# A decoder layer on one core: masked maximum on VectorE instead of a mask matmul, and a new order of VectorE's, ScalarE's and GpSimd's turn

## The chip, the core and the metric

The program runs on one core of one Trainium2 chip. A core has a matrix engine (TensorE, "PE" in the rows, with its weight loads as "PEld"), a vector engine (VectorE, DVE), a scalar engine (ScalarE, ACT), GpSimd (POOL) and a sync engine (SP) that only issues transfers here. The engines run side by side, each works through its own instructions in order, and they wait for one another by semaphores. The metric is the device time of one execution in microseconds.

## The reference

The input is `x` of 2 x 1024 x 512. The layer is an attention block and a gated feed-forward block, each between two layer norms and a residual:

```
xn = layernorm(x)                       # 2048 rows of 512
q = xn @ Wq (32 heads x 128); k, v = xn @ Wk, xn @ Wv (8 heads x 128, each shared by 4 q heads)
o_lin = gla_scan(softmax(q), softmax(k), v, logsigmoid(k)/16)    # linear attention with decay
y = sliding window attention (64 back, in blocks of 64, positions rotated), masked softmax
o = bf16(0.5*y + 0.5*o_lin) @ Wo;  x = x + layernorm(o)
w1, w2, w3 -> NF4 quantised and dequantised, in blocks of 64 with their absolute maximum
h = silu(xn @ w1') * (xn @ w2');  x = x + layernorm(h @ w3')
```

The masked softmax sets scores outside the window to minus infinity, takes each row's maximum, subtracts it, and normalises the exponentials by their sum.

## The kernel before

The 2048 rows are 16 tiles of 128. One **turn** handles one tile and one k/v head with its 4 q heads, so there are 128 turns, in 32 groups of four; `p` = 0, 1, 2, 3 is the turn's place in its group. Groups 0 to 3 and 28 to 31 are written out, groups 4 to 27 are the body of a loop. After the turns comes the feed-forward block, which the change leaves alone.

Each engine has a function `turn(t)` that writes its instructions in a fixed order; it works on turn t and also on pieces of the turns before (`l1` = t-1, `l2` = t-2, `l3` = t-3). `wait_tile(engine, semaphore, turn, back)` is the wait for a turn's step.

TensorE's order in a turn: `project_kv(t)`, `decays_and_krT(l1)`, `project_out(l3)`, `gla_scores(l2)`, `turn_q(l1)`, `inter_and_update(l2)`, `probabilities(l2)`, `scores(l1)`, `project_q(t)`, `qsT_and_ktT(l1)`, `output(l2)`. `scores` first writes the window's mask (0 or -1e30) into the bank SC by a matmul of `win` with an identity, and adds the four score products to it. `project_kv(t)` overwrites the bank PKV, and waits for `kabs_ev` and `gl_d` of turn t-1, the last reads of that bank.

VectorE's order in a turn: `use_k(t)` (maximum, minimum with zero and rotation of k), `q_sums(l1)`, `gla_k(l1)`, `merge(l2)`, `add_out(l3)`, `state(l2)`, `p_max(l1)` (the maximum of the scores, once `scores` is done), `log_decay(t)` (writes `gh` and PKV), `low_decay(t)` (writes `gl`, signals `gl_d`), the NF4 work, `p_sums(l1)`, `use_q(t)`, `gla_q(l1)`.

The NF4 work turns the feed-forward weights into quantised ones, one piece of 128 x 512 per group. `nf4_blocks` finds the maximum of each block of 64 and its reciprocal; `nf4` divides (`f_nrm`) and then writes 15 steps `f_s[k % 8]` = (f_nrm > bound_k) * delta_k; GpSimd adds the 15 steps up in `f_acc` (`nf4_add`, one turn later); `nf4_end` scales the sum. `NF4_STEPS` says which k come in which turn of a group.

GpSimd's order in a turn: `rotate_q(l1)`, `rotate_k(t)`, `softmax_q(l1)`, `nf4_add(l1)`, `softmax_p(l1)`, `split_low` (the low halves of the next weights; the 512-wide one where p = 3).

ScalarE copies banks out and takes exponentials; of its order the change touches `q_exps(l1)` (exponentials of q, needed by `project_q(t)`) and `decays(l1)` (needed by `gla_k`, signals `dec_ev`).

Of the kernel before, what the change touches and what calls it, by code (L numbers as in the profile page):

```python
# [45 lines left out]
NF4_STEPS = (range(0, 2), range(2, 6), range(6, 11), range(11, 15))  # L46
# [63 lines left out]
def layer(nc, x, wq, wk, wv, wo, wf, cosc, sinc, winmask, causal, cumsum, identc, keepc, dq, out):  # L110
# [15 lines left out]
    with ExitStack() as whole:  # L126
# [10 lines left out]
        def sb(name, shape, dt=F32):  # L137
# [76 lines left out]
        rp = sb("rp", [P, 2, GRP])  # L214
        f_max = sb("f_max", [P, 2, NF4_MAX // BLK])
# [30 lines left out]
            rp_d pm_d pa_ev su_d em_d sr_d acc_d qrope_p krope_p qn_p pn_p  # L246
# [198 lines left out]
        def _(pool):  # L445
# [31 lines left out]
            def nf4_add(t):  # L477
                w = width_of(t.i)
                for k in NF4_STEPS[t.p]:
# [16 lines left out]
            def turn(t):  # L496
# [24 lines left out]
            nf4_add(last_turn)  # L521
# [23 lines left out]
        def _(act):  # L545
# [20 lines left out]

            def q_exps(t):
# [12 lines left out]
            def decays(t):  # L580
# [7 lines left out]
                nc.scalar.activation(edT[:, r, :], SM[:, P:P + 130], ACT.Exp)  # L588
                nc.scalar.activation(ked, ked, ACT.Exp, scale=-1.0).then_inc(s["dec_ev"], 1)
# [101 lines left out]
            def turn(t):  # L691
# [13 lines left out]
                k_exps(t)  # L705
                if n == 0:
# [103 lines left out]
        def _(dve):  # L810
# [30 lines left out]

            def low_decay(t):
# [188 lines left out]
            def turn(t):  # L1031
                l1, l2, l3, n = t.back(1), t.back(2), t.back(3), number(t)
                use_k(t)
                if l1.real():
                    q_sums(l1)
# [35 lines left out]
                if t.p == 0:  # L1071
                    nf4(t)
# [76 lines left out]
            state(l2)  # L1149
# [30 lines left out]
        def _(pe):  # L1180
# [84 lines left out]
            def scores(t):  # L1265
# [4 lines left out]
                nc.tensor.matmul(SC[:], identb[:], win[:, 1, :] if t.p else win[:, t.i % 2, :], start=True, stop=False)  # L1270
                low = 1 - r
                for b in range(2):
# [3 lines left out]
                    for hp in range(2):  # L1276
# [3 lines left out]
                                                start=False, stop=(j == 3))  # L1280
# [167 lines left out]
def constants():  # L1448
# [37 lines left out]
    keep = np.ones((P, 2), np.float32)  # L1486
    keep[:, 0] = 0.0
# [21 lines left out]
```

## Time and profile before

| | |
|---|---|
| time, median of 3 runs | 1959.39 us (1958.69 to 1960.08) |
| the profiled execution, its own time | 1959.31 us |
| its span from the first to the last instruction | 1957.5 us |
| busy in the span: PE, DVE, ACT, POOL | 1876.3, 1433.4, 1229.4, 1235.9 us |
| granted TensorE clock, mean | 0.99 |

The whole execution is 1.8 us longer than its span. A busy figure is the time in which at least one instruction of an engine was under way. A timeline row gives the start, how long the instruction (or a merged run of "xN" of them) was under way, the engine, the line of the kernel, the operation, what it writes and reads, and in brackets an idle time ahead of it with what ended that. Successive instructions of an engine overlap: what one costs its engine is the distance to the next start, not its own length. A TensorE product of two fp32 operands shows as two matmul records.

### The profile page before, as it was taken

The page shows a single profiled execution, that of the slowest core. Times are in us where ns is not written, and L with a number is a line of the kernel's source. Part 1 is how long each engine was busy: PE and PEld are TensorE (multiplying, and loading weights), DVE is VectorE, ACT ScalarE, POOL GpSimd, SP SyncE. Part 2 cuts the span into 40 slices and gives each one's busy share as a digit, 9 for nine tenths or more (in the row PEclk, how much of TensorE's full clock was granted, in tenths as well). Part 3 has the DMA queues.
Part 4 walks back from the last instruction along what each step waited for, and adds up shares of the span by engine and source line. Part 5 has one row for each costly group of instructions (what it writes and reads, how often), then busy time and mean ns, then how long its engine had stood idle before and what let it go on. Part 6 is the DMA issues. An engine that isn't in the chain of part 4 may idle for free.

```text
span 1957.5 us, 42161 instructions
## 1 busy us (share of the span) xinstructions
PE 1876.3 (96%) x11698; PEld 1252.8 (64%) x11698; DVE 1433.4 (73%) x3926; ACT 1229.4 (63%) x4840; POOL 1235.9 (63%) x1150
## 2 busy tenths in 40 slices
PE   4999999999999999999999999999989979999997
PEld 3667677777777777776777676777666635444443
DVE  6998888888888888888888888888899644302022
ACT  5777777777777777777777777776666535312121
POOL 3777777777777777777777777777677521212121
PEclk8999999999999999999999999999999989999999
DMA  5000000000000000000000000000100042000000
GB/s 199 25 26 25 26 25 24 24 24 24 32 25 24 24 24 24 29 24 24 24 24 24 30 29 24 24 24 13 54 13 7 7 134 79 26 1 22 0 21 21
DMA packets 44353, 61.43 MB, mean 31 GB/s; under 512 B 4928, under 2 KB 18496, under 8 KB 44288
## 3 DMA queue, kind: packets, MB, share of 16 engines
q1 hardware_dynamic: 44288, 60.64, 9.6%
q8 instruction: 32, 0.52, 0.1%
q14 instruction: 33, 0.27, 0.0%
HBM read 47.97 MB, written 12.65 MB: 31 GB/s over the span
## 4 chain that ended last, share of the span: by engine, by line
PE 62%; DVE 16%; issue 14%; POOL 3%; ACT 2%; DVEq 1%; DMA 0%; SPq 0%; POOLq 0%; ACTq 0%
PE bank L1250 18%; PE bank L1239 8%; PE bank L1278 6%; PE bank L1221 4%; PE bank L1294 4%; PE bank L1315 4%; PE bank L1379 3%; PE bank L1287 3%; DVE f_s L963 2%; PE bank L1205 2%; PE bank L1304 2%; POOL hl L527 2%; DVE f_nrm L953 2%; PE bank L1270 1%; PE bank L1297 1%
## 5 line engine op out<-in xcount | busy, mean ns | idle before, releaser
L488 POOL TENSOR_TENSOR f_acc<-f_acc,f_s 128x512 f32<-128x512 f32 (+1 forms) x416 | 534.3, 1284 | 30.6 <-POOL f_acc L488 0.4
L1250 PE MATMUL bank<-wh,xh 128*128 (+2 forms) x1024 | 334.9, 327 | 7.3 <-DVE cumh L1099 6.2
L1250 PE MATMUL bank<-wl,xh 128*128 (+2 forms) x1024 | 335.0, 327 | 0.0
L1250 PE MATMUL bank<-wh,xl 128*128 (+2 forms) x1024 | 334.7, 327 | 0.0
L469 POOL TENSOR_TENSOR pr<-pr,rp 128x512 f32<-128x512 f32 x128 | 133.0, 1039 | 229.5 <-DVE rp L894 229.5
L963 DVE TENSOR_SCALAR f_s<-f_nrm 128x512 f32<-128x512 f32 (+1 forms) x480 | 240.9, 561 | 3.7
L575 ACT ACTIVATE qe<-bank,nqm 128x128 f32<-128x128 f32 x512 | 180.8, 365 | 80.3 <-DVE qs L823 57.2
L527 POOL TENSOR_TENSOR hl<-hf,hh 128x512 f16<-128x512 f32 (+1 forms) x44 | 50.8, 1155 | 283.7 <-ACT hh L754 283.7
L1379 PE MATMUL bank<-xh,w 128*128 (+3 forms) x704 | 224.8, 382 | 3.8 <-ACT sg L748 3.8
L603 ACT ACTIVATE pr<-bank,pmx 128x128 f32<-128x128 f32 x512 | 180.9, 367 | 37.5 <-DVE pmx L887 29.6
L1239 PE MATMUL bank<-wh,oT 128*128 (+1 forms) x512 | 194.0, 379 | 3.8 <-DVE xl L1019 1.4
L1239 PE MATMUL bank<-wl,oT 128*128 (+1 forms) x512 | 194.0, 379 | 0.0
L1109 DVE SCALAR_TENSOR_TENSOR hf<-bank,sg 128x512 f32<-128x512 f32 (+1 forms) x44 | 30.4, 690 | 215.8 <-PE bank L1379 203.3
L594 ACT ACTIVATE qrT<-bank 128x512 f32<-128x512 f32 x128 | 76.4, 597 | 170.1 <-PE bank L1205 170.1
L451 POOL TENSOR_TENSOR qc<-qc,qs 128x512 f32<-128x512 f32 x128 | 162.9, 1273 | 23.3 <-DVE qs L823 23.3
L456 POOL TENSOR_TENSOR kc<-kc,ks 128x128 f32<-128x128 f32 x128 | 72.2, 564 | 117.0 <-DVE ks L823 117.0
L1250 PEld LDWEIGHTS bank<-wh,xl 128*128 (+1 forms) x1024 | 100.5, 98 | 66.9 <-issue 0.8
L1250 PEld LDWEIGHTS bank<-wl,xh 128*128 (+1 forms) x1024 | 100.5, 98 | 66.5 <-issue 0.6
L887 DVE TENSOR_REDUCE pmx<-bank 128x4 f32<-128x512 f32 x128 | 88.2, 689 | 73.1 <-PE bank L1278 73.1
L1250 PEld LDWEIGHTS bank<-wh,xh 128*128 (+1 forms) x1024 | 100.8, 98 | 61.6 <-issue 8.9
L1278 PEld LDWEIGHTS bank<-krT,qrT 128*128 128x128 f32 x1024 | 135.3, 193 | 4.9
L1278 PE MATMUL bank<-krT,qrT 128*128 128x128 f32 x1024 | 135.8, 276 | 0.0
(177 smaller groups left out, 4973.7 us busy)
## 6 DMA issues: line engine op xcount, KB each, us to landing
f_raw<-wf SPq DMA_DIRECT2D x30, 256.0 KB, 2.6
dequantised<-f_dq SPq DMA_DIRECT2D x30, 256.0 KB, 2.0
wt<-dequantised SPq DMA_DIRECT2D x30, 256.0 KB, 3.0
raw_qkv<-wq SPq DMA_DIRECT2D x29, 256.0 KB, 2.5
raw_o<-wo SPq DMA_DIRECT2D x29, 256.0 KB, 2.6
rows<-x SPq DMA_DIRECT2D x4, 1024.0 KB, 9.3
xr<-x SPq DMA_DIRECT2D x16, 256.0 KB, 3.6
out<-yo SPq DMA_DIRECT2D x16, 256.0 KB, 2.1
```

Source lines behind the costliest of these rows:

```text
L451: nc.gpsimd.tensor_tensor(qc[:, r, :], qc[:, r, :], qs[:, r, :], ALU.add).then_inc(s["qrope_p"], 1)
L469: nc.gpsimd.tensor_tensor(v, v, rp[:, r, :].unsqueeze(2).to_broadcast([P, GRP, P]), ALU.mult).then_inc(s["pn_p"], 1)
L488: nc.gpsimd.tensor_tensor(f_acc[:, 0:w], f_acc[:, 0:w], f_s[:, k % 8, 0:w], ALU.add)\
L527: nc.gpsimd.tensor_tensor(hl[0:n, c % 2, :], hf[0:n, c % 2, :], hh[0:n, c % 2, :], ALU.subtract)\
L575: last = nc.scalar.activation(qe[:, r, h * P:(h + 1) * P], PQ[:, h * P:(h + 1) * P], ACT.Exp, bias=nqm[:, r, h:h + 1], scale=1.0 / WSCALE, ...
L603: last = nc.scalar.activation(pr[:, r, j * P:(j + 1) * P], SC[:, j * P:(j + 1) * P], ACT.Exp, bias=pmx[:, r, j:j + 1], accum_out=psm[:, r, ...
L887: nc.vector.tensor_reduce(pmx[:, r, :], SC[:].rearrange("p (h n) -> p h n", h=GRP), AX.X, ALU.max, negate=True).then_inc(s["pmx_d"], 1)
L963: nc.vector.tensor_scalar(f_s[:, k % 8, 0:w], f_nrm[:, 0:w], float(BOUND[k]), float(DELTA[k]), ALU.is_gt, ALU.mult).then_inc(s["f_sd"], 1)
L1239: last = nc.tensor.matmul(PW[:], oT[:, t.p % 2, h].rearrange("p b n -> p (b n)"), w[:, sl + h, QW + KVW:WW], start=(h == 0 and k == 0), st ...
L1250: last = nc.tensor.matmul(dst, av, w[:, sl + c, lo:hi], start=(n == 0), stop=(n == 3 * NC - 1))
L1278: last = nc.tensor.matmul(SC[:, j * P:(j + 1) * P], qrT[:, r, b, 2 * hp:2 * hp + 2, :].rearrange("p h n -> p (h n)"), keys, start=False, s ...
L1379: last = nc.tensor.matmul(dst[0:n, :], w12[c][:, ww, "gu".index(kind), d, 0:n], x4, start=(k == 0), stop=(k == 3 * NC - 1))
```

## The change

1. TensorE no longer multiplies the mask into SC. The first score product starts the bank. VectorE's `p_max` is no longer one reduction over 128 x 512 but, after a one-element memset, four instructions over 128 x 128 that each compute `-(scores + mask)`, write it back to SC and keep the smallest value as `pmx`; each comes with a read-out of that value. ScalarE's exponential then uses scale -1. In turns with p = 0 the mask of the first two heads is `win0`, a copy that ScalarE makes in the same turn (`head_mask`).
2. VectorE's turn: `q_sums(l1)` moves behind `add_out`; `state(l2)` is cut in two, and `state_scale` moves behind `p_max`; the reciprocal of k's sums (`k_sums`) moves from `gla_k(l1)` to the turn before; `low_decay(t)` moves behind `nf4(t)`; `nf4_blocks(i + 1)` comes in the turn with p = 1 of group i, and `nf4` of the turn with p = 0 takes the same place as in the others.
3. `em`, the factor that clears the state where a sequence starts, is made by ScalarE's exponential with a bias, not by a VectorE product.
4. ScalarE: `decays(l1)` ahead of `q_exps(l1)`.
5. GpSimd: the first two additions of `nf4_add(l1)` ahead of `softmax_q(l1)`.
6. `NF4_STEPS` becomes 2, 3, 5, 5 steps in place of 2, 4, 5, 4.

```diff
-NF4_STEPS = (range(0, 2), range(2, 6), range(6, 11), range(11, 15))
+NF4_STEPS = (range(0, 2), range(2, 5), range(5, 10), range(10, 15))
...
                 if l1.real():
+                    nf4_add(l1, NF4_STEPS[l1.p][:2])
                     softmax_q(l1)
-                    nf4_add(l1)
+                    nf4_add(l1, NF4_STEPS[l1.p][2:])
                     softmax_p(l1)
...
+            def head_mask(t):
+                if t.p == 0:
+                    nc.scalar.activation(win0[:], win[:, t.i % 2, 0:P], ACT.Copy).then_inc(s["head_mask"], 1)
...
                 nc.scalar.activation(edT[:, r, :], SM[:, P:P + 130], ACT.Exp)
+                if t.p == 0 and not (isinstance(t.i, int) and t.i == 0):
+                    nc.scalar.activation(em[:, 0, :], SM[:, 2 * P:2 * P + 1], ACT.Exp,
+                                         bias=keep[:].unsqueeze(2)[:, t.i % 2, :])
...
 -                                                bias=pmx[:, r, j:j + 1],
+                                                bias=pmx[:, r, j:j + 1], scale=-1.0,
...
                 if l1.real():
+                    decays(l1)
                     q_exps(l1)
-                    decays(l1)
...
+            def k_sums(t):
+                r = t.p % 2
+                wait_tile(dve, s["ke_ev"], t)
+                nc.vector.reciprocal(rks[:, r, :], ksum[:, r, :]).then_inc(s["rks_d"], 1)
...
-                nc.vector.tensor_reduce(pmx[:, r, :], SC[:].rearrange("p (h n) -> p h n", h=GRP), AX.X, ALU.max,
-                                        negate=True).then_inc(s["pmx_d"], 1)
+                nc.vector.memset(pause[:], 0.0)
+                for j in range(GRP):
+                    sl = slice(j * P, (j + 1) * P)
+                    mask = win[:, 1, sl] if t.p or j >= 2 else win0[:]
+                    last = nc.vector.tensor_tensor_reduce(SC[:, sl], SC[:, sl], mask, -1.0, -MASKED, ALU.add,
+                                                          ALU.min, pmx[:, r, j:j + 1])
+                last.then_inc(s["pmx_d"], 1)
...
                 use_k(t)
-                if l1.real():
-                    q_sums(l1)
...
+                if l1.real():
+                    q_sums(l1)
                 if l2.real():
-                    state(l2)
+                    state_sum(l2)
                 if l1.real():
                     p_max(l1)
+                if l2.real():
+                    state_scale(l2)
                 log_decay(t)
+                k_sums(t)
+                if t.p == 0 and isinstance(t.i, int) and t.i == 0:
+                    nf4_blocks(0)
+                nf4(t)
                 low_decay(t)
-                if t.p == 0:
-                    nf4_blocks(t.i)
-                else:
-                    nf4(t)
+                if t.p == 1 and not (isinstance(t.i, int) and t.i == STEPS - 1):
+                    nf4_blocks(t.i + 1)
...
-                nc.tensor.matmul(SC[:], identb[:], win[:, 1, :] if t.p else win[:, t.i % 2, :], start=True, stop=False)
+                if t.p == 0:
+                    pe.wait_ge(s["head_mask"], t.i + 1)
...
-                                                start=False, stop=(j == 3))
+                                                start=(j == 0), stop=(j == 3))
```

VectorE from `state` to `p_sums` in a turn that has five steps, before (`sr` is the scaled state, `pmx` the maximum, `gh` and `gl` the high and low half of the log decay, `f_s` the NF4 steps, `rp` the reciprocal of the probabilities' sums):

```order
L911 TENSOR_TENSOR bank<-bank,sr 128x128 [waits s_u_done]
L922 TENSOR_SCALAR sr<-bank,edT 128x128 [waits s_su_d,s_dec_ev]
L887 TENSOR_REDUCE pmx<-bank 128x4 [waits s_sc_done]
L839 TENSOR_TENSOR gh<-bank,kabs 128x128 [waits s_small_done,s_kneg_d,s_l1_ev]
L840 TENSOR_TENSOR bank<-bank,kabs 128x128
L845 TENSOR_TENSOR gl<-bank,gh 128x128 [waits s_g_d]
L963 TENSOR_SCALAR f_s<-f_nrm 128x512 [waits s_f_ad] x5
L894 RECIPROCAL rp<-psm 128x4 [waits s_pn_p,s_p_exp]
```

And in the changed kernel, in the same kind of turn, from the third of the four masked maxima on:

```order
L907 ISA pmx 128x1
L907 ISA bank,pmx<-bank,win 128x128
L907 ISA pmx 128x1
L944 TENSOR_SCALAR sr<-bank,edT 128x128 [waits s_su_d,s_dec_ev]
L851 TENSOR_TENSOR gh<-bank,kabs 128x128 [waits s_small_done,s_kneg_d,s_l1_ev]
L852 TENSOR_TENSOR bank<-bank,kabs 128x128
L857 RECIPROCAL rks<-ksum 128x1 [waits s_ke_ev]
L985 TENSOR_SCALAR f_s<-f_nrm 128x512 [waits s_f_ad] x5
L862 TENSOR_TENSOR gl<-bank,gh 128x128 [waits s_g_d]
L915 RECIPROCAL rp<-psm 128x4 [waits s_pn_p,s_p_exp]
```

`gl` stood three rows behind the maximum and ahead of the five steps. It now stands behind them, and `sr` and `rks` stand between the maximum and the steps.

GpSimd's turn with p = 0 before (`kc` and `qc` are rotations, `qe` is the normalised exponentials of q, `pr` those of the scores, `f_acc` the NF4 sum):

```order
L456 TENSOR_TENSOR kc<-kc,ks 128x128 [waits s_krope_d]
L462 TENSOR_TENSOR qe<-qe,rq 128x512 [waits s_rq_d]
L488 TENSOR_TENSOR f_acc<-f_acc,f_s 128x512 [waits s_f_ad,s_f_sd] x4
L469 TENSOR_TENSOR pr<-pr,rp 128x512 [waits s_rp_d]
L475 TENSOR_TENSOR wl<-raw_qkv,wh 128x256 [waits s_wqk_hi]
```

And after:

```order
L453 TENSOR_TENSOR qc<-qc,qs 128x512 [waits s_qrope_d]
L458 TENSOR_TENSOR kc<-kc,ks 128x128 [waits s_krope_d]
L490 TENSOR_TENSOR f_acc<-f_acc,f_s 128x512 [waits s_f_ad,s_f_sd] x2
L464 TENSOR_TENSOR qe<-qe,rq 128x512 [waits s_rq_d]
L490 TENSOR_TENSOR f_acc<-f_acc,f_s 128x512 [waits s_f_ad,s_f_sd] x3
L471 TENSOR_TENSOR pr<-pr,rp 128x512 [waits s_rp_d]
```

Two additions stand ahead of `qe`, three behind it; the turn with p = 0 has five additions where it had four.

## Rows read from the trace of the kernel before

**Rows 1.** Engine totals over 1000 us of the middle: busy us (count), clock.

```profile
400.00:1400.00 1000.00, 992.28 (x6576) 708.43 (x6575) 850.32 (x2413) 722.25 (x3070) 769.00 (x723) 1.00 0.08 26
```

**Rows 2.** TensorE timeline, a turn with p = 3: start us, us, engine, line, tiles.

```profile
1008.73 0.38 PE L1270 MATMUL bank<-win,identb 128*128 128x512 bf16 x1
1008.94 1.05 PE L1278 MATMUL bank<-krT,qrT 128*128 128x128 f32 x8
1009.83 0.38 PE L1250 MATMUL bank<-wh,xh 128*128 x1
...
1013.83 0.27 PE L1250 MATMUL bank<-wh,xh 128*128 x1
...
1021.33 0.38 PE L1250 MATMUL bank<-wh,xh 128*128 x1
```

**Rows 3.** TensorE timeline, the turn with p = 1.

```profile
1030.21 1.02 PE L1294 MATMUL bank<-qtT,sr 128*128 128x512 f32 x2
1031.51 0.49 PE L1297 MATMUL bank<-va,kt 128*128 128x128 f32 x2 [0.28 <-DVE kt L862]
...
1033.64 0.38 PE L1250 MATMUL bank<-wh,xh 128*128 x1
```

**Rows 4.** VectorE timeline, the same turn with p = 3.

```profile
1010.03 0.69 DVE L887 TENSOR_REDUCE pmx<-bank 128x4 f32<-128x512 f32 x1 [0.72 <-PE bank L1278]
1010.64 0.28 DVE L839 TENSOR_TENSOR gh<-bank,kabs 128x128 f16<-128x128 f32 x1
1010.84 0.29 DVE L840 TENSOR_TENSOR bank<-bank,kabs 128x128 f32<-128x128 f32 x1
1011.16 0.29 DVE L845 TENSOR_TENSOR gl<-bank,gh 128x128 f16<-128x128 f32 x1
...
1014.21 0.17 DVE L894 RECIPROCAL rp<-psm 128x4 f32<-128x4 f32 x1
1014.30 0.65 DVE L850 TENSOR_REDUCE qmx<-bank 128x4 f32<-128x512 f32 x1
...
1017.46 0.21 DVE L823 TENSOR_TENSOR ks<-bank,sin 128x64 f32<-128x64 f32 x1
```

**Rows 5.** VectorE timeline, two of its four `f_s`, from windows that hold one each.

```profile
1011.37 0.83 DVE L963 TENSOR_SCALAR f_s<-f_nrm 128x512 f32<-128x512 f32 x1
...
1012.12 1.50 DVE L963 TENSOR_SCALAR f_s<-f_nrm 128x512 f32<-128x512 f32 x1
```

**Rows 6.** GpSimd timeline, the turn with p = 3 and the start of p = 0.

```profile
1005.19 0.45 POOL L456 TENSOR_TENSOR kc<-kc,ks 128x128 f32<-128x128 f32 x1 [0.19 <-DVE ks L823]
1005.60 1.04 POOL L462 TENSOR_TENSOR qe<-qe,rq 128x512 f32<-128x512 f32 x1
1006.60 6.74 POOL L488 TENSOR_TENSOR f_acc<-f_acc,f_s 128x512 f32<-128x512 f32 x5
1014.46 1.04 POOL L469 TENSOR_TENSOR pr<-pr,rp 128x512 f32<-128x512 f32 x1 [1.12 <-DVE rp L894]
1015.45 1.16 POOL L475 TENSOR_TENSOR wl<-raw_o,wh 128x512 f32 x1
1016.57 1.27 POOL L451 TENSOR_TENSOR qc<-qc,qs 128x512 f32<-128x512 f32 x1
...
1026.76 1.27 POOL L451 TENSOR_TENSOR qc<-qc,qs 128x512 f32<-128x512 f32 x1 [0.17 <-DVE qs L823]
```

**Rows 7.** VectorE timeline, `f_nrm` of two groups in a row.

```profile
980.39 1.38 DVE L953 TENSOR_TENSOR f_nrm<-f_raw,f_rec 128x512 f32<-128x512 f32 x1
...
1027.20 1.38 DVE L953 TENSOR_TENSOR f_nrm<-f_raw,f_rec 128x512 f32<-128x512 f32 x1
```

**Rows 8.** VectorE timeline, the turn with p = 1 of the earlier group.

```profile
986.79 0.41 DVE L922 TENSOR_SCALAR sr<-bank,edT,em 128x128 f32<-128x128 f32 x1
987.12 0.68 DVE L887 TENSOR_REDUCE pmx<-bank 128x4 f32<-128x512 f32 x1
...
988.45 1.42 DVE L963 TENSOR_SCALAR f_s<-f_nrm 128x512 f32<-128x512 f32 x4
```

More of the change, by code:

```diff
@@ L214, in layer @@
         rp = sb("rp", [P, 2, GRP])
+        pause = sb("pause", [P, 1])
+        win0 = sb("win0", [P, P], BF16)
         f_max = sb("f_max", [P, 2, NF4_MAX // BLK])
@@ L245, in layer @@
             kmx_d nkm_a kabs_ev kneg_d krope_d g_d gl_d rks_d kt_d qmx_d nqm_a qrope_d rq_d qt_d pmx_d
-            rp_d pm_d pa_ev su_d em_d sr_d acc_d qrope_p krope_p qn_p pn_p
+            rp_d pm_d pa_ev su_d head_mask sr_d acc_d qrope_p krope_p qn_p pn_p
             wqk_sc wqk_hi wqk_lo wo_sc wo_hi wo_lo w0_hi raw_a raw_b consts z_id
@@ L475, in split_low, with nf4_add @@
                 nc.gpsimd.tensor_tensor(wl[:, job % 8, lo:hi], src, wh[:, job % 8, lo:hi], ALU.subtract).then_inc(low, 1)
-            def nf4_add(t):
+            def nf4_add(t, steps):
                 w = width_of(t.i)
-                for k in NF4_STEPS[t.p]:
+                for k in steps:
                     pool.wait_ge(s["f_sd"], t.i * 15 + (k + 1))
@@ L520, in _ @@
             softmax_p(last_turn)
-            nf4_add(last_turn)
+            nf4_add(last_turn, NF4_STEPS[last_turn.p])
             def low_hidden(g, c):
@@ L705, in turn @@
                 k_exps(t)
+                head_mask(t)
                 if n == 0:
@@ L857, in gla_k @@
                 wait_tile(dve, s["ke_ev"], t)
-                nc.vector.reciprocal(rks[:, r, :], ksum[:, r, :]).then_inc(s["rks_d"], 1)
                 wait_tile(dve, s["rks_d"], t)
@@ L905, in merge, with state_sum, state_scale @@
                                                op0=ALU.max, op1=ALU.add).then_inc(s["pm_d"], 1)
-            def state(t):
-                r, nxt = t.p % 2, t.back(-1)
+            def state_sum(t):
+                r = t.p % 2
                 wait_tile(dve, s["u_done"], t)
                 nc.vector.tensor_tensor(su, SM[:, 0:P], sr[:, r, :], ALU.add).then_inc(s["su_d"], 1)
+            def state_scale(t):
+                r, nxt = t.p % 2, t.back(-1)
                 if not nxt.real():
@@ L916, in state @@
                 if nxt.p == 0:
-                    nc.vector.tensor_tensor(em[:, 0, :], scale, keep[:, nxt.i % 2:nxt.i % 2 + 1] if isinstance(nxt.i, int)
-                                            else keep[:].unsqueeze(2)[:, nxt.i % 2, :], ALU.mult).then_inc(s["em_d"], 1)
-                    dve.wait_ge(s["em_d"], nxt.i)
                     scale = em[:, 0, :]
@@ L1070, in turn @@
                     gla_q(l1)
-                if t.p == 0:
-                    nf4(t)
                 if n in (2, 6):
@@ L1148, in _ @@
             add_out(l3)
-            state(l2)
+            state_sum(l2)
+            state_scale(l2)
             p_max(l1)
@@ L1485, in constants @@
     cum /= 16.0
-    keep = np.ones((P, 2), np.float32)
-    keep[:, 0] = 0.0
+    keep = np.zeros((P, 2), np.float32)
+    keep[:, 0] = MASKED
     return {"cosc": cos, "sinc": sin, "winmask": win, "causal": cau, "cumsum": cum,
```

1 line of the change is left out of this document (removed).

## Prediction

> **What bounds the kernel now.** First the totals of a stretch in the middle: TensorE is busy 992 of 1000 us at full clock, VectorE 850, GpSimd 769, ScalarE 722 [rows 1]. So TensorE's own work sets the time, and what it waits for on top is small. Then one turn on TensorE, in its timeline [rows 2]: scores end and `project_q` starts at 1009.83, the next `project_kv` at 1013.83, the next `project_q` at 1021.33. A turn is 11.50 us without a gap. In the turn with p = 1 it is 12.31 (1021.33 to 1033.64) [rows 2, 3]: there `kt` is late, and TensorE stands still for 0.81 between the state product at 1030.21 and the transposes. A group is 3 x 11.50 + 12.31 = 46.81, and `f_nrm`, which comes once per group, returns after 46.81 [rows 7]. 31 such distances make up nearly all of the turns.
>
> The third view is VectorE beside GpSimd. VectorE starts `p_max` 0.20 after the scores end, `gl` comes 1.13 behind that, and only then the NF4 steps [rows 4]. A clean step costs 0.335 (four in 1.42, the last one 0.415 long) [rows 8]. In this turn VectorE has four steps, and two of them are 0.83 and 1.50 long [rows 5]. GpSimd's five additions start every (6.74 - 1.34) / 4 = 1.35 [rows 6]; the fourth ends near 1011.92, the fifth near 1013.34, and the long steps end at 1012.20 and 1013.62, 0.28 after each. So a step that meets an addition begins only about 0.13 before that addition's recorded end; and when an addition was waiting, it got in between two steps. `f_nrm` does the same behind `qc` (1.38 long, it ends 0.55 after `qc`) [rows 6, 7], while instructions with one operand in PSUM, and the small reciprocals, keep their length. The Trainium skill states this rule: SBUF — State Buffer, section "Who interferes with whom", says that a VectorE instruction in a two-port mode or with two SBUF inputs and a GpSimd instruction lock each other out whole. The trace agrees, with the 1.50 above. By that rule the masked maximum (one input in PSUM) is not locked out.
>
> **The change part by part.** I count from K, the start of `project_kv`, and from S, the start of `p_max`. TensorE reaches `project_kv` of the next turn at S + 3.80 (4.00 - 0.20) [rows 2, 4], and it must have `gl` of this turn by then.
>
> TensorE loses the mask product: 1008.94 - 1008.73 = 0.21 per turn [rows 2]. A turn without waits is 11.29, a group 45.16.
>
> The wait for `kt` in the turn with p = 1 (0.81) goes: the decays come ahead of q's exponentials, the reciprocal is taken a turn earlier, and `f_nrm` no longer stands just ahead of that turn. `ks` ends at K + 3.33 (below), `f_dq` and `kt` follow by about K + 4.2, and TensorE asks for `kt` at K + 5.7, so 1.5 is to spare.
>
> The masked maximum is in no row. A 128-column instruction on a bank costs 0.20 to the next start (1010.64 to 1010.84), a small one 0.09 (1014.21 to 1014.30) [rows 4]. The memset and four pairs make 0.09 + 4 x 0.29 = 1.25, against 0.61 now. The lower end is that same 0.61; the upper is each length taken whole, 0.29 and 0.17, which gives 0.1 + 4 x 0.46 = 1.94. I take 1.25, since the other instructions of these shapes do overlap. The Trainium skill (VectorE: DVE Perf Modes, section on the TRN2 errata) has 120 + 128 cycles at 0.96 GHz for such a form, 0.26; with that as the distance, an estimate would be 1.49 and the sum some 7 us more. The trace has 0.20 as the distance and 0.28 as the length.
>
> Behind the maximum now come `sr` (0.33, 986.79 to 987.12) [rows 8], `gh` and its partner 0.40, `rks` 0.10. The first NF4 instruction is therefore ready at S + 1.25 + 0.83 = S + 2.08. Behind the steps comes `gl`, whose end reaches TensorE 0.34 after its start (length 0.29 and 0.05 of signalling). This is the new wait, and what is queued behind it is all of TensorE.
>
> - p = 1, three steps: 2.08 + 1.00 + 0.34 = 3.42. No wait.
> - p = 2, five steps: 2.08 + 1.68 + 0.34 = 4.10. TensorE waits 0.30. GpSimd has three additions there and is done by then.
> - p = 3, five steps while GpSimd has five additions. Where do these stand? `gl` starts 0.34 before K when TensorE waits for it, `rp` follows 0.21 later, `ks` is 3.25 behind `rp` and 0.21 long [rows 4], and 0.08 after it GpSimd can take `kc`: K + 3.41. S is K + 7.50 - 0.21 + 0.20 = K + 7.49, so `kc` starts at S - 4.08. Then 0.41, two additions, `qe` (1.00), three additions [rows 6]: the fourth runs from S + 1.37 to 2.64, the fifth from 2.72 to 3.99. The first step (ready at 2.08) waits until 2.51, the fifth addition slips in, the second step waits 1.13 more. `gl` is at TensorE at 2.08 + 0.43 + 1.13 + 1.68 + 0.34 = 5.66. Wait: 1.86.
> - p = 0, `f_nrm` (0.80 with the wait behind it) and two steps, again with five additions. GpSimd's queue (`pr` 0.25 after `rp`, then 0.99, 1.12 and 1.22) puts `kc` at the same place within 0.05 [rows 6]. 2.08 + 0.45 + 1.14 + 0.80 + 0.67 + 0.34 = 5.48. Wait: 1.68.
>
> Sum: 45.16 + 0.30 + 1.86 + 1.68 = 49.00 per group, 2.19 more than 46.81. Times 31 it is +68. The profiled execution took 1959.31 (span 1957.5 and 1.8 around it), as good as the median of 1959.39, so the forecast is 2027.
>
> The bounds of the masked maximum move this little. With 0.61 the wait of p = 2 goes, but the two collisions stay, since the step waits for the same addition: 48.7, 2018. With 1.94 the waits are 0.32, 0.99, 2.08 and 1.87: 50.4, 2071.
>
> Costed at nothing: ScalarE's `em` and `win0` (0.1 and 0.3 per group, on an engine with 28% idle); q's exponentials up to 0.6 later, done near K + 4.2, where `project_q` needs them at K + 7.3; `qe` 2.7 later on GpSimd, done near K + 7.6, where TensorE transposes it at K + 9.9; `nf4_blocks`, about 1.0, behind `gl` in the turn that has room. VectorE loses the 1.4 us `f_nrm` collision of its old place, but it was idle in three turns of four anyway. If `qe`'s cover were gone, TensorE would wait at its transposes in the two heavy turns, a few tenths each.
>
> **The rivals.**
>
> *The additions don't meet the steps* (faster). If GpSimd finished its five additions before S + 2.08, or if they met without a lock, the waits would be 0.30 in p = 2 and 3 and 0.10 in p = 0: 45.86 per group, 31 x -0.95 = -29, 1930. For it: the lock was never on TensorE's path before, so nothing there shows its effect on the time. Against it: GpSimd would have to start `kc` 1.8 us earlier, and `kc` hangs on VectorE work that starts only behind `gl`. It decides itself at this point: fifth addition over before the first step.
>
> *One collision and not two* (no change). If VectorE kept the port for its whole burst, only 0.43 to 0.45 would be added in p = 3 and 0: waits 0.30, 0.73, 0.55; 46.74 per group, 1957. Against it is the second long step, 1.50, in the trace [rows 5].
>
> *The masked maximum is dear*. It is a special instruction that no row shows. At 0.65 per pair it takes 2.69, the first step is ready at S + 3.52, and all four turns wait: 1.06, 1.74, and behind one collision of 0.34 then 2.08 and 1.87; 51.9 per group, 2117. For it speaks only that it is unseen; against it, that every VectorE row of this width lies at 0.20 to 0.33.
>
> *The change doesn't do what it says*, with `kt` late as before: it would add 0.8 to a group that waits anyway for `gl` later in the turn; it would show as 2050.
>
> **How the numbers follow.** The forecast has 0.67, no collisions 0.13, one collision 0.09, the dear maximum 0.08, the last 0.03. The range goes from 1955 (it takes in the case of one collision) to 2070 (the forecast's own span, about 2005 to 2071). What a measurement of this kernel can tell from no change is about 0.2%, 4 us: faster 0.15 (no collisions, and some of one collision), same 0.05, slower 0.80.
>
> **What would show it.** In the new trace TensorE waits at the first product of `project_kv` for VectorE's `gl`, about 1.9 and 1.7 us in two turns of a group, 0.3 in a third; no mask product; `kt` not waited for. VectorE has one step per heavy turn that is about 1.5 us long and another of 0.8. A group is 49.0. The forecast is wrong if the additions end before the steps begin, or if TensorE waits somewhere else, above all for the probabilities or `qtT`, which would tell that VectorE's load and not the place of `gl` decides. A masked maximum far from 0.30 per head would move the sum as above.

## The result, and the profile after

The changed kernel takes 2048.02 us (median of 4 runs, 2046.56 to 2050.97), 1.0454 times the kernel before, with a 95% interval of 1.0436 to 1.0472. The forecast was 2027 with a range of 1955 to 2070: the direction, the place and most of the size were right; 21 us were missing.

The first view is again the totals of the stretch from 400 to 1400 us (the columns of [rows 1]):

```profile
400.00:1400.00 1000.00, 944.84 (x6087) 653.67 (x6085) 781.79 (x2882) 686.79 (x2920) 728.03 (x682) 0.98 0.08 24
```

The list of what TensorE waited for in the same stretch (us in total, times, longest) has one entry:

```profile
PE bank L1275 <- DVE gl L862: 54.4, 40, 1.8
```

TensorE is busy 47 us less in 1000 than in [rows 1], and the granted clock is 0.98 where it was 1.00. The wait for `kt` [rows 3] is gone; `project_kv` (L1275) waits for `gl`, 40 times in 20 groups. From one group's first k maximum to the next it is 49.96 us on average (46.80 before).

TensorE's timeline from a turn with p = 3 into the next group, and then one turn later:

```profile
1019.28 0.59 PE L1341 MATMUL bank<-pa,va 128*128 128x256 f32 x2
1021.66 0.28 PE L1275 MATMUL bank<-wh,xh 128*128 x1 [1.79 <-DVE gl L862]
1021.78 0.27 PE L1275 MATMUL bank<-wl,xh 128*128 x1
1021.89 0.27 PE L1275 MATMUL bank<-wh,xl 128*128 x1
1022.16 0.28 PE L1275 MATMUL bank<-wh,xh 128*128 x1
...
1023.28 0.42 PE L1275 MATMUL bank<-wh,xh 128*128 x1
1023.50 0.42 PE L1275 MATMUL bank<-wl,xh 128*128 x1
...
1023.92 0.31 PE L1220 MATMUL bank<-gh,cumh 128*128 128x128 f16 x1
...
1024.57 0.63 PE L1264 MATMUL bank<-wh,oT 128*128 x1
...
1026.98 0.22 PE L1239 MATMUL bank<-cau,identb 128*128 128x128 bf16 x1
...
1034.46 0.59 PE L1341 MATMUL bank<-pa,va 128*128 128x256 f32 x2
1035.99 0.28 PE L1275 MATMUL bank<-wh,xh 128*128 x1 [0.94 <-DVE gl L862]
...
1037.30 0.22 PE L1220 MATMUL bank<-gh,cumh 128*128 128x128 f16 x1
```

The matmuls of `output` end their issue 0.43 after 1019.28; `project_kv` starts 1.94 behind that, and 1.10 in the next turn. Three things are to be seen beside the waits. In the second place the twelve products of `project_kv` take 1.31 us (1035.99 to 1037.30), as they do where nothing waits. In the first they take 2.26: after every third product there is a hole (1021.89 to 1022.16, where 0.11 is the clean distance), and from about 1022.67 on the products follow one another at twice the distance. The second effect shows in the granted clock of the same stretch (same columns as above):

```profile
1022.00:1023.00 1.00, 0.99 (x7) 0.61 (x6) 1.00 (x4) 0.00 (x0) 1.00 (x2) 0.77 0.00 0
1023.00:1024.00 1.00, 1.00 (x7) 0.63 (x6) 0.66 (x2) 0.00 (x0) 1.00 (x2) 0.50 0.00 0
1024.00:1025.00 1.00, 1.00 (x8) 0.66 (x7) 0.83 (x5) 0.19 (x2) 0.69 (x1) 0.50 0.47 37
1025.00:1026.00 1.00, 1.00 (x4) 0.45 (x3) 0.40 (x2) 0.97 (x8) 0.81 (x2) 0.53 0.59 225
1026.00:1027.00 1.00, 1.00 (x7) 0.41 (x5) 0.07 (x1) 1.00 (x7) 0.92 (x2) 1.00 0.00 0
```

The clock is at its lower level (0.50, 1.2 GHz) for about 3.4 us, from shortly after TensorE takes up work again. It costs 0.19 in `project_kv` (2.26 against 2.07), 0.31 in the decays (0.65 against 0.34) and 0.68 in `project_out` (2.41 against 1.73), 1.2 us in all; it happens behind the long wait in two groups of three.

VectorE in the same two turns:

```profile
1015.92 0.29 DVE L907 CUSTOM_DVE_ANT_0 bank<-bank,win 128x128 f32<-128x128 f32 x1 [1.04 <-issue]
1015.94 0.06 DVE L903 MEMSET pause<- 128x1 f32 x1
1016.13 0.14 DVE L907 DVE_READ_ACCUMULATOR2_ANT pmx<- 128x1 f32 x1
1016.13 0.33 DVE L907 CUSTOM_DVE_ANT_0 bank<-bank,win 128x128 f32<-128x128 f32 x1
...
1016.87 0.41 DVE L944 TENSOR_SCALAR sr<-bank,edT 128x128 f32<-128x128 f32 x1
...
1017.66 3.28 DVE L985 TENSOR_SCALAR f_s<-f_nrm 128x512 f32<-128x512 f32 x5
1020.87 0.28 DVE L862 TENSOR_TENSOR gl<-bank,gh 128x128 f16<-128x128 f32 x1
...
1031.10 0.29 DVE L907 CUSTOM_DVE_ANT_0 bank<-bank,win 128x128 f32<-128x128 f32 x1 [1.04 <-issue]
...
1032.84 0.94 DVE L975 TENSOR_TENSOR f_nrm<-f_raw,f_rec 128x512 f32<-128x512 f32 x1
1033.92 1.61 DVE L985 TENSOR_SCALAR f_s<-f_nrm 128x512 f32<-128x512 f32 x2
1035.45 0.28 DVE L862 TENSOR_TENSOR gl<-bank,gh 128x128 f16<-128x128 f32 x1
```

S is again the start of the maximum (1015.92 in p = 3, 1031.10 in p = 0). The masked maximum takes 1016.87 - 1015.92 = 0.95, an instruction with its read-out 0.25. In p = 3 five steps take 3.28, where clean ones take 4 x 0.335 + 0.415 = 1.76: 1.52 for the two collisions. In p = 0 it is 2.61 from `f_nrm` to `gl`, where clean work takes 0.80 + 0.67 = 1.47: 0.26 for `f_nrm` and 0.86 for a step. GpSimd beside it, in p = 3 and then in p = 0:

```profile
1015.62 4.04 POOL L490 TENSOR_TENSOR f_acc<-f_acc,f_s 128x512 f32<-128x512 f32 x3
...
1025.61 2.61 POOL L490 TENSOR_TENSOR f_acc<-f_acc,f_s 128x512 f32<-128x512 f32 x2
1029.62 1.04 POOL L464 TENSOR_TENSOR qe<-qe,rq 128x512 f32<-128x512 f32 x1 [1.40 <-DVE rq L898]
1030.62 4.29 POOL L490 TENSOR_TENSOR f_acc<-f_acc,f_s 128x512 f32<-128x512 f32 x3
```

In p = 3 the additions end at 1015.62 + 4.04 = 1019.66, S + 3.74. In p = 0 GpSimd's first two additions come early, at S - 5.49, but then `qe` waits 1.40 for `rq` (`q_sums` stands behind `add_out` now), and the last three additions stand against VectorE nearly where they do in p = 3: from S - 0.48 to S + 3.81. There `f_nrm` meets the fourth addition and the first step the fifth. Behind `f_nrm` VectorE has a wait of 0.14 in any case, which here runs while the fifth addition is under way.

### The profile page after: what moved, and what is told of

Its sections match the earlier page's. It is cut to its first block, busy times and chain, and to the rows that moved or that the text cites. A ratio compares the mean times of both kernels' runs of the same rounds, so it can differ in the third digit from the quotient of the medians.

```text
span 2044.2 us, 43142 instructions
## 1 busy us (share of the span) xinstructions
PE 1890.4 (92%) x11570; PEld 1235.5 (60%) x11570; DVE 1415.8 (69%) x4919; ACT 1242.9 (61%) x4903; POOL 1244.2 (61%) x1150
## 4 chain that ended last, share of the span: by engine, by line
PE 64%; issue 17%; DVE 13%; ACT 2%; POOL 2%; DVEq 1%; DMA 1%; SPq 0%; POOLq 0%; ACTq 0%
PE bank L1275 20%; PE bank L1264 11%; PE bank L1246 5%; PE bank L1320 5%; DVE f_s L985 4%; PE bank L1304 4%; PE bank L1341 3%; PE bank L1405 3%; PE bank L1230 3%; PE bank L1313 2%; PE bank L1330 2%; POOL hl L530 2%; PE bank L1323 1%; PE bank L1423 1%; DVE pmx L907 1%
## 5 line engine op out<-in xcount | busy, mean ns | idle before, releaser
L490 POOL TENSOR_TENSOR f_acc<-f_acc,f_s 128x512 f32<-128x512 f32 (+1 forms) x416 | 544.1, 1308 | 21.3
L1275 PE MATMUL bank<-wh,xh 128*128 (+2 forms) x1024 | 339.3, 331 | 102.4 <-DVE gl L862 96.2
L1275 PE MATMUL bank<-wh,xl 128*128 (+2 forms) x1024 | 339.3, 331 | 0.0
L1275 PE MATMUL bank<-wl,xh 128*128 (+2 forms) x1024 | 338.8, 331 | 0.0
L985 DVE TENSOR_SCALAR f_s<-f_nrm 128x512 f32<-128x512 f32 (+1 forms) x480 | 262.8, 606 | 3.6
L907 DVE CUSTOM_DVE_ANT_0 bank<-bank,win 128x128 f32<-128x128 f32 x512 | 132.9, 321 | 134.9 <-issue 134.9
L1275 PEld LDWEIGHTS bank<-wh,xh 128*128 (+1 forms) x1024 | 100.9, 99 | 203.0 <-issue 152.0
L1264 PE MATMUL bank<-wh,oT 128*128 (+1 forms) x512 | 203.5, 397 | 0.0
L1264 PE MATMUL bank<-wl,oT 128*128 (+1 forms) x512 | 201.7, 394 | 0.0
L591 ACT ACTIVATE krT<-bank 128x64 f32<-128x64 f32 x128 | 28.7, 224 | 267.8 <-PE bank L1223 267.8
L464 POOL TENSOR_TENSOR qe<-qe,rq 128x512 f32<-128x512 f32 x128 | 133.4, 1042 | 52.6 <-DVE rq L898 52.5
L1275 PEld LDWEIGHTS bank<-wh,xl 128*128 (+1 forms) x1024 | 101.6, 99 | 68.9 <-issue 1.1
L1246 PE MATMUL bank<-ktT,qtT 128*128 128x64 f32 (+1 forms) x1024 | 135.3, 275 | 0.0
```

Source lines behind the costliest of these rows:

```text
L464: nc.gpsimd.tensor_tensor(v, v, rq[:, r, :].unsqueeze(2).to_broadcast([P, GRP, P]), ALU.mult).then_inc(s["qn_p"], 1)
L490: nc.gpsimd.tensor_tensor(f_acc[:, 0:w], f_acc[:, 0:w], f_s[:, k % 8, 0:w], ALU.add)\
L907: last = nc.vector.tensor_tensor_reduce(SC[:, sl], SC[:, sl], mask, -1.0, -MASKED, ALU.add, ALU.min, pmx[:, r, j:j + 1])
L985: nc.vector.tensor_scalar(f_s[:, k % 8, 0:w], f_nrm[:, 0:w], float(BOUND[k]), float(DELTA[k]), ALU.is_gt, ALU.mult).then_inc(s["f_sd"], 1)
L1246: last = nc.tensor.matmul(X1[:, j * P:j * P + keys], qtT[:, r, b, 2 * hp:2 * hp + 2, :].rearrange("p h n -> p (h n)"), ktT[:, r, 0:keys], ...
L1264: last = nc.tensor.matmul(PW[:], oT[:, t.p % 2, h].rearrange("p b n -> p (b n)"), w[:, sl + h, QW + KVW:WW], start=(h == 0 and k == 0), st ...
```

## The experiments

Each ran beside the kernel before on one chip. The group length is the steady one of the loop, the mean of a step that of the stretch from 400 to 1400 us. "Clean" work of TensorE in a group is 45.16 us without the mask product and 46.00 with it.

| run | time, us | ratio to before | group, us | mean `f_s`, ns |
|---|---|---|---|---|
| before | 1959.45 | | 46.80 | 528 |
| changed | 2048.02 | 1.0454 (1.0436 to 1.0472) | 49.96 | 573 |
| gl_first | 1963.98 | 1.0021 (1.0011 to 1.0031) | 46.74 | 645 |
| mask_matmul | 2033.63 | 1.0376 (1.0358 to 1.0393) | 49.40 | 568 |
| maximum_alone | 1971.17 | 1.0054 (1.0037 to 1.0071) | 47.11 | 593 |
| additions_undone | 2193.05 | 1.1184 (1.1165 to 1.1203) | 54.61 | 867 |
| short_additions | 1933.39 | 0.9870 (0.9854 to 0.9887) | 46.63 | 419 |
| gl_behind | 2003.27 | 1.0225 (1.0208 to 1.0242) | 48.52 | 586 |
| steps_0555 | 1992.80 | 1.0173 (1.0156 to 1.0190) | 47.60 | 632 |
| steps_0654 | 1990.45 | 1.0158 (1.0141 to 1.0175) | 47.50 | 706 |
| even_3444 | 1920.29 | 0.9792 (0.9779 to 0.9806) | 45.33 | 619 |
| even_4344 | 1913.04 | 0.9754 (0.9740 to 0.9767) | 45.15 | 446 |
| even_product | 1936.76 | 0.9875 (0.9860 to 0.9890) | 46.00 | 527 |
| behind_4344 | 1972.58 | 1.0065 (1.0048 to 1.0081) | 47.34 | 452 |

The theory after the result was: `gl` behind the steps is what costs, and the steps are made long by meeting additions. The rivals were the masked maximum, VectorE's load as such, and the additions' own place.

**gl_first**

```diff
-                nf4(t)
                 low_decay(t)
+                nf4(t)
```

> The changed kernel with low_decay (gl) put back ahead of the NF4 steps; everything else as changed. Theory (the place of gl behind the steps is what costs): the waits of TensorE for gl, 3.2 us of a group of 49.95 us, are gone from its waits. If nothing else is late then, a group is 45.2 to 46.8 us (the matmul work alone, or the measured group less the waits), 1897 to 1947 us in all. Rival (the steps hold up q's maximum and rope as well, which stand behind them in either order): TensorE waits for qt at the GLA scores instead, 47 to 48.5 us a group, 1953 to 2000 us. Second rival (the steps are not what gl waits for): 2040 us or more.

84 of the 89 us are gone with two lines exchanged. The rest goes to the first rival (46.74 us a group is a little under its 47 to 48.5, 1963.98 us lies inside its 1953 to 2000); TensorE's list has one entry, and it is now for `qt`:

```profile
PE bank L1239 <- DVE qtT L888: 27.7, 43, 1.6
```

The steps are longer here than in the changed kernel (645 ns on average), but what stands behind them is needed later. Per group the waits for `qt` are 0.65 and 0.91 us, and 45.16 + 1.56 = 46.72 is the group. So the product saved and the `kt` wait saved (1.65 a group) are nearly paid back by these.

**mask_matmul** (the mask product and the single reduction again, all orders as changed; `head_mask`, the scale of -1 and the new start of the bank go with the masked maximum)

```diff
+                nc.tensor.matmul(SC[:], identb[:], win[:, 1, :] if t.p else win[:, t.i % 2, :], start=True, stop=False)
...
-                nc.vector.memset(pause[:], 0.0)
-                for j in range(GRP):
-                    ...
-                    last = nc.vector.tensor_tensor_reduce(...)
+                nc.vector.tensor_reduce(pmx[:, r, :], SC[:].rearrange("p (h n) -> p h n", h=GRP), AX.X, ALU.max, negate=True)
```

> The changed kernel with the old masking: the mask product on TensorE and one reduce on VectorE; the orders on all engines as changed. Theory (the order costs, the masked maximum hardly anything): TensorE works 0.21 us more in each turn, 0.84 us a group; the reduce takes 0.69 us where the four masked maxima take 0.96, so gl comes 0.27 us earlier in the two turns that wait for it, 0.54 us a group less. Sum +0.3 us a group, 2048 to 2060 us. Rival (the masked maximum itself is what makes it slower): 1960 to 2000 us.

The masked maximum isn't the cause, so much held. But the kernel is 14 us faster than the changed one, not as slow or slower. The waits for `gl` show it in part: they are 1.60 and 0.88 us and none in p = 2, where the changed kernel has 1.94, 1.10 and 0.14. That is 0.70 a group and not the 0.54 that I counted: to the start of what follows it, the reduction takes 0.61 and the masked maximum 0.95, so 0.34 lie between them and not 0.27. The rest is the clock: the stretch has 1.00 where the changed kernel has 0.98, and no fall to 0.50.

```profile
400.00:1400.00 1000.00, 955.18 (x6241) 670.79 (x6240) 765.09 (x2273) 699.13 (x2940) 736.85 (x689) 1.00 0.08 24
```

**maximum_alone** (the kernel before with part 1 of the change only; `win0` and `head_mask` added, the product out)

> The kernel before with the masked maximum alone; every order as before. Theory (TensorE bounds, VectorE has 0.3 us to spare where nothing waits for gl): a turn 11.50 less 0.21 us, 45.9 to 46.2 us a group with the wait for kt kept, 1931 to 1941 us. Rival (the 0.27 us that VectorE takes longer pass on to q's maximum and to qt, and TensorE waits at the GLA scores): 47 to 48 us a group, 1966 to 1996 us.

The rival holds, at its lower edge. TensorE now has two waits:

```profile
PE bank L1311 <- DVE kt L870: 16.3, 20, 0.8
PE bank L1227 <- DVE qtT L880: 9.2, 21, 0.5
```

The `kt` wait is that of [rows 3], untouched: with the old orders it stays, and in no kernel with the new ones does it show. The `qt` wait is new; VectorE had not even this 0.34 us (0.95 less 0.61) to spare in its old order.

**additions_undone**

```diff
-                    nf4_add(l1, NF4_STEPS[l1.p][:2])
                     softmax_q(l1)
-                    nf4_add(l1, NF4_STEPS[l1.p][2:])
+                    nf4_add(l1, NF4_STEPS[l1.p])
```

> The changed kernel with all NF4 additions of a turn behind q's normalisation on GpSimd again. Theory (the two early additions are one of the two that meet the NF4 steps on VectorE, at a price of 0.43 us in one turn and 0.45 in another, and qe is what they delay): the additions start later and fall on the later steps of VectorE instead, and pr waits behind all of them, so that the probabilities are late: 2045 to 2130 us. Rival (the early additions cost by their collisions only): the collisions of 1.6 us in each of two turns halve, 2000 to 2030 us.

Even the theory's upper end was too low. A step takes 867 ns on average, and TensorE waits for `gl` up to 3.7 us:

```profile
PE bank L1274 <- DVE gl L861: 131.0, 55, 3.7
```

With `qe` first, all additions come late: `qe` waits 2.36 us for `rq` in p = 3 and 3.93 in p = 0, and the additions behind it run when VectorE makes its steps, so that in p = 3 four steps in a row are stretched, three of them to 1.5 us. So the two early additions are the good part of the change: they are worth 145 us at the place where `gl` stands.

**short_additions** (the changed kernel with 7/8 of each addition left out, so its sums are incomplete)

```diff
-                        nc.gpsimd.tensor_tensor(f_acc[:, 0:w], f_acc[:, 0:w], f_s[:, k % 8, 0:w], ALU.add)\
+                        nc.gpsimd.tensor_tensor(f_acc[:, 0:w // 8], f_acc[:, 0:w // 8], f_s[:, k % 8, 0:w // 8], ALU.add)\
...
```

> The changed kernel, gl still behind the NF4 steps, with GpSimd's NF4 additions on the first eighth of the columns only (this leaves 7/8 of the additions out); VectorE does all its steps. Theory (of the two long waits for gl, the collisions with additions are the part that decides): the maximum takes 0.96 us, the first step is ready at S + 1.79, no step is longer than 0.42, gl comes at TensorE at S + 3.81 in p = 2 and 3 and at S + 3.60 in p = 0, against the 3.80 that TensorE allows; 45.2 to 45.7 us a group, 1897 to 1915 us, and no fall of TensorE's clock. Rival (VectorE's load and the place of gl cost by themselves): waits for gl of 0.3 us and more in three turns, 46.5 us a group and more, 1940 us or above.

The mean step is as long as a clean one and none is longer than 0.46, and 115 us go: the collisions carry the loss. GpSimd's queue is emptier here too, but in the changed kernel VectorE stood idle ahead of its steps for only 2.8 us of the whole stretch, so what goes is their length and no wait of theirs. But a group is 46.63, not 45.2 to 45.7: the rival's 46.5 and more, though the time stayed under its 1940. TensorE's timeline into a new group shows what the theory lacked:

```profile
768.87 0.59 PE L1342 MATMUL bank<-pa,va 128*128 128x256 f32 x2
769.72 0.28 PE L1276 MATMUL bank<-wh,xh 128*128 x1 [0.26 <-issue]
...
769.95 0.27 PE L1276 MATMUL bank<-wh,xl 128*128 x1
770.22 0.28 PE L1276 MATMUL bank<-wh,xh 128*128 x1
...
771.21 0.28 PE L1276 MATMUL bank<-wh,xh 128*128 x1
...
771.79 0.23 PE L1221 MATMUL bank<-gh,cumh 128*128 128x128 f16 x1
```

`project_kv` starts only 0.42 late (769.72 against 768.87 + 0.43), yet takes 2.07 instead of 1.31, at full clock. Every fourth product begins about 0.50 after the one three before it, where the clean distance is 0.33. The trace's records of TensorE's own queue hold two register operations at each of these holes, and two more between the semaphore and the first weight load; their line is that of these products, and I read them as working out the address of the weights' slot. The slot changes with the group, and in the other turns the trace has one where it has two here. In kernels in which TensorE isn't held at the semaphore these records lie ahead, beside earlier matmuls, and there are no holes; where it is held, they come one by one behind it. From the start of `gl` to the first product it is 0.79 us at this place (1020.87 to 1021.66 above) and 0.54 in the next turn (1035.45 to 1035.99), not 0.34. A `gl` that is only just late costs some 0.75 us more at the first turn of a group.

**gl_behind** (the kernel before, `gl` behind the steps)

```diff
-                low_decay(t)
                 if t.p == 0:
                     nf4_blocks(t.i)
                 else:
                     nf4(t)
+                low_decay(t)
```

> The kernel before with gl behind the NF4 steps and nothing else changed. Theory (the place costs only what the steps ahead of it overrun): gl is at TensorE at S + 1.01 + 2.84 + 0.34 = S + 4.19 in p = 3 (four steps, two of them 0.83 and 1.50 us long) against 3.80, a wait of 0.4 us in one turn of four; none in the others. 46.8 to 47.3 us a group, 1960 to 1976 us. Rival (the place costs in itself, in every turn): 49 us a group, 2025 us and more.

Between theory and rival. TensorE waits in one turn of four, as expected:

```profile
PE bank L1250 <- DVE gl L845: 25.4, 21, 1.3
```

but for 1.39 us, not 0.4. The first step of p = 3 is 1.40 long, where the expectation had 0.83 (GpSimd's fourth addition now ends 2.11 after the start of the maximum, and 1.89 before), and from `gl` to the first product it is 0.80 and not 0.34. With the restart of 0.76, 46.00 + 1.39 + 0.76 = 48.15 of 48.52.

**steps_0555 and steps_0654** (the changed kernel with `gl` ahead of the steps, `nf4_blocks` in p = 0 again; the second has 0, 6, 5, 4 steps)

```diff
-NF4_STEPS = (range(0, 2), range(2, 5), range(5, 10), range(10, 15))
+NF4_STEPS = (range(0, 0), range(0, 5), range(5, 10), range(10, 15))
```

> The changed kernel with gl ahead of the steps, the block maxima back in the turn p = 0, and the NF4 steps of a group spread as 0, 5, 5, 5 over its four turns in place of 2, 3, 5, 5. Theory (what is left of the waits are those for qt behind colliding steps, 0.75 us in the turn of p = 0 and 0.49 in that of p = 3): the first is gone, since no step meets an addition there; 45.6 to 46.0 us a group, 1925 to 1940 us. Rival (VectorE is full, so that what leaves one turn holds up another): 46.5 to 47.5 us a group, 1955 to 1985 us.

> As the run with 0, 5, 5, 5 but with the steps spread as 0, 6, 5, 4. Theory: the turn of p = 3, in which two steps meet additions, has one clean step less, 0.34 us, so its wait for qt falls from 0.49 to 0.15; the turn of p = 1 has room for six. 45.3 to 45.7 us a group, 1915 to 1932 us. Rival (six steps are too many for the turn with f_dq in it): a new wait of 0.3 us or more there, as slow as 0, 5, 5, 5 or slower.

Both theories failed, and the times lie at or above the rivals' ranges; the 0.3 us and more that the second rival expected behind six steps did not come there. There are more collisions, not fewer, five a group where gl_first has four: five steps in p = 3 take 3.91, and `f_nrm` takes 1.60 and the 128 x 8 `f_safe` 0.68 where 0.17 is its clean length:

```profile
1030.41 3.91 DVE L985 TENSOR_SCALAR f_s<-f_nrm 128x512 f32<-128x512 f32 x5
1043.79 0.68 DVE L966 SCALAR_TENSOR_TENSOR f_safe<-f_max 128x8 f32 x1
...
1044.74 1.60 DVE L975 TENSOR_TENSOR f_nrm<-f_raw,f_rec 128x512 f32<-128x512 f32 x1
```

Taking the steps out of a turn with five additions doesn't help, since the additions remain and meet what is there; and steps bunched in one turn make five additions in the next. The waits for `qt` (1.33, 0.83 and 0.25 us in 0, 5, 5, 5) give 45.16 + 2.41 = 47.57.

**even_3444 and even_4344** (as gl_first, with the additions spread evenly)

```diff
-NF4_STEPS = (range(0, 2), range(2, 5), range(5, 10), range(10, 15))
+NF4_STEPS = (range(0, 4), range(4, 7), range(7, 11), range(11, 15))
```

> The changed kernel with gl ahead of the steps and the steps of a group spread as 3, 4, 4, 4 over its four turns in place of 2, 3, 5, 5, all else as in the run gl_first. GpSimd then has 2, 4, 4 and 4 additions in the turns p = 1, 2, 3, 0 in place of 1, 3, 5, 5. Theory (TensorE waits for qt only where q's maximum starts more than 4.8 us after the masked maximum; gl_first has 5.25 in p = 3 and 5.52 in p = 0, and a turn with four additions meets one step and not two): p = 3 loses a step and a collision, p = 0 gains a step and loses a collision, both come to 4.4 to 5.0, and the waits of 0.65 and 0.91 us go but for 0 to 0.3 us. 45.2 to 45.6 us a group, 1915 to 1935 us, faster than the kernel before. Rival (with four additions and four steps p = 2 gets a collision and a wait of its own, as in the run with 0, 5, 5, 5): 46.5 us a group or more, 1955 us or above.

> As even_3444 with the steps spread as 4, 3, 4, 4, that is one step moved from p = 1 to p = 0 and one addition from the turn p = 2 to p = 1. Theory: p = 0 comes to 5.1 to 5.3 and keeps a wait of 0.3 to 0.5 us, p = 2 meets no addition. 45.5 to 45.9 us a group, 1925 to 1940 us. Rival (the collision in p = 2 is what costs in even_3444): faster than even_3444.

Both are faster than the kernel before, and 4, 3, 4, 4 is the fastest of all, 2.5% below it. The order between the two went to the rival, though not quite as it had it. 3, 4, 4, 4 has a whole collision in p = 2 and one in p = 3, and TensorE waits behind neither. The 0.18 us that it keeps fall in p = 0, where the first step is 1.27 long and `qt` comes late: the additions of that turn stand about 1.0 later against `gl` than in 4, 3, 4, 4. That the collisions ahead of it held GpSimd up by so much is my reading. In 4, 3, 4, 4 the additions are over, or nearly, when the steps begin. VectorE in p = 3 and p = 0:

```profile
1027.24 0.29 DVE L862 TENSOR_TENSOR gl<-bank,gh 128x128 f16<-128x128 f32 x1
1027.45 1.49 DVE L985 TENSOR_SCALAR f_s<-f_nrm 128x512 f32<-128x512 f32 x4
...
1038.74 0.87 DVE L975 TENSOR_TENSOR f_nrm<-f_raw,f_rec 128x512 f32<-128x512 f32 x1
1039.75 1.43 DVE L985 TENSOR_SCALAR f_s<-f_nrm 128x512 f32<-128x512 f32 x4
```

GpSimd's last two additions of the same turns:

```profile
1025.04 2.61 POOL L490 TENSOR_TENSOR f_acc<-f_acc,f_s 128x512 f32<-128x512 f32 x2
...
1036.44 2.61 POOL L490 TENSOR_TENSOR f_acc<-f_acc,f_s 128x512 f32<-128x512 f32 x2
```

They end at 1027.65 and 1039.05, 0.20 and 0.31 after the start of the first step or of `f_nrm`; four clean steps are 1.42. TensorE's group of 45.15 is its clean work.

**even_product** (even_3444 with the mask product and the single reduction)

> As even_3444 with the old masking: the product on TensorE and one reduce on VectorE. Theory (once TensorE bounds, the masked maximum is worth the product, 0.21 us a turn): TensorE works 46.0 us a group, VectorE is 0.27 us a turn less late, no waits; 10 to 25 us slower than even_3444, 1935 to 1950 us. Rival (VectorE's time decides also there): as fast as even_3444 or faster.

As expected: 46.00 a group, which is the work with the product. Against even_3444 the masked maximum is worth 16 us.

**behind_4344** (the changed kernel with the spread 4, 3, 4, 4 alone)

> The changed kernel with nothing but the spread of the steps altered, 4, 3, 4, 4 in place of 2, 3, 5, 5; gl stays behind them. Theory (gl behind the steps costs what the steps overrun, so with hardly any collision left the place is cheap): p = 1 and 2 need 3.5 us from the start of the maximum and less, p = 3 has four steps with a meeting of 0.3 us, 3.7 to 3.8 us, all within the 3.80 that TensorE allows; p = 0 needs 1.79 + 0.80 + 4 x 0.335 + 0.34 = 4.27, a wait of 0.47 us. 45.6 to 45.9 us a group, 1927 to 1937 us. Rival (the wait of p = 0 shifts the additions against the steps, and a whole collision of 1.1 us comes back in p = 3, with the slow restart of 0.75 us behind it): 1.1 - 0.3 + 0.75 us more, 47 to 48.5 us a group, 1970 to 2015 us.

Neither. The time lies inside the rival's range, but by luck: no whole collision comes back (a step 0.68 long is the worst of a steady group), so its mechanism is wrong. But the waits are 0.35 and 0.92, with the restart of 0.76 behind the first: 45.16 + 2.03 = 47.19. In p = 3 `gl` starts 3.35 after the maximum, and I had counted 0.34 and not 0.79 from there to TensorE's product.

## Why the prediction was right, and where 21 us came from

- *The product goes, 0.21 a turn*: right; 45.15 a group in even_4344.
- *The wait for `kt` goes*: right. It is in maximum_alone (old orders) and in no kernel with the new ones. Which of the three edits named does it wasn't tried apart.
- *The masked maximum, 1.25 us*: too high, 0.95. An instruction with its read-out costs 0.25 and not 0.29. The Trainium skill (VectorE: DVE Perf Modes, section on the TRN2 errata) has 120 + 128 cycles, 0.26, for an instruction of 128 columns that reads PSUM. The trace's 0.25 agrees, but for the pair as a whole: the read-out, 0.14 long, lies beside the next instruction and is not to be added, as the estimate of 1.49 had done. As the prediction said, it hardly moves the time: the steps end with the additions, not earlier.
- *`gl` reaches TensorE 0.34 after its start*: this step failed. The figure was `gl`'s length and 0.05 of signalling, and it holds as far as TensorE's queue, which records the semaphore 0.32 after the start of `gl`. But from there to the first product it takes 0.22 more in p = 0 and 0.47 more into a new group, for which the sum had nothing: 0.54 and 0.79 in all.
- *p = 3, wait 1.86*: 1.94 measured, by two errors that cancel. `gl` started at S + 4.95, not S + 5.32 (the last addition ended at S + 3.74 and not 3.99), and needed 0.79 from there and not 0.34.
- *The two collisions, 0.43 + 1.13*: right, 1.52. short_additions shows them as the cause. This is the rule of the Trainium skill (SBUF — State Buffer, "Who interferes with whom"); its rows here are the mean step of 419 ns with short additions and 867 ns with all of them late, and the masked maximum, which ran beside an addition and kept its 0.33 us.
- *p = 0, wait 1.68*: 1.10. Both collisions came, but cheaper: 0.26 + 0.86 in place of 0.45 + 1.14. The fourth addition ended at S + 2.14 and not 2.64, the maximum was shorter, and the price of 1.14 was that of two steps in a row, where the 0.14 of waiting behind `f_nrm` overlaps the addition. That the last additions stood where they do in p = 3 was right by luck: the prediction had `kc` at the same place in both, and it came 1.6 earlier in p = 0 (S - 5.91 and S - 4.29), which `qe`'s wait of 1.40 for `rq`, foreseen nowhere, nearly made up.
- *p = 2, wait 0.30*: 0.14.
- *Not in the sum*: the slow restart, 0.75 a group, and the fall of the clock, 1.2 in two groups of three, 0.8.

The waits come to 3.18 and not 3.84; 45.16 + 3.18 + 0.75 + 0.8 = 49.89 of the 49.96 of a group. So the forecast came as near as it did partly by luck: it had 0.66 too much of waiting, and lacked 1.55 of what comes with a wait. Against 49.00 the group is 0.96 more, and 0.96 x 31 is 30 us; the written-out groups lost less than the 3.2 us of a steady one (the first took 51.08 and 50.25 before), so that 21 are left. The restart is measured in four other kernels at full clock: 2.02 to 2.09 us for `project_kv`, in mask_matmul, short_additions, gl_behind and behind_4344. That the queue's register operations are its cause is read from the trace and wasn't tested. Why the clock falls in the changed kernel (after 1.94, in two groups of three) and in additions_undone (after 3.9), and not in mask_matmul (1.60) or gl_behind (1.39), was not tested either. The length of the wait alone doesn't decide it: the second wait of a group in additions_undone is 2.17 long and no fall follows it.

Of the rivals, *no collisions* is what short_additions makes: it gave 1933 where the rival said 1930, though with a group of 46.63 and not 45.86; the written-out groups, where the kernel before also loses to collisions, make up for it (the first took 47.60 and 50.25 before). *One collision* and *the dear maximum* are refuted by the rows above, and so is the last rival, since `kt` isn't waited for.

## What to carry to other kernels

A small instruction that another engine waits for belongs ahead of work that can be stretched by a third engine: exchanging two lines was worth 84 us here, more than the 51 us (1.65 in each of 31 groups) that the product and the `kt` wait together could give. Where VectorE and GpSimd share work in bursts, spread it so that one's burst is over when the other's begins; the same change with `gl` first and the steps 4, 3, 4, 4 runs in 1913 us, 2.5% faster than before. And price a new wait with what stands behind its release: addresses that the waiting queue could have worked out ahead, and the clock.

## What the hardware showed beside this

- TensorE held at a semaphore restarted slowly where its queue had register operations among the next products: 0.79 us from the start of the releasing instruction, and 2.07 us for twelve products that otherwise take 1.31.
- After waits of 1.94 us (two groups of three) and 3.9 us (each group) the granted clock fell to 0.50 for about 3.4 us, soon after work was taken up again; after one of 2.17 us it did not.
- A 128 x 8 instruction of VectorE with its operands in SBUF was held back beside a GpSimd addition as a large one is: 0.68 us and not 0.17.
- A masked minimum over 128 x 128 with one operand in PSUM, its read-out included, cost 0.25 us to the next one's start.
